# Input transposes, keys and queries of a batch five steps earlier, across the batch boundary

## The chip, the cores and the metric

The kernel runs on one core of a Trainium2 chip. The metric is the time on the device, in microseconds (us), and the median over runs. The kernel before takes 2675.65 us (three runs, 2670.8 to 2685.03).

## The reference

One transformer layer in float32 on x of 16 batches x 512 tokens x 256 features. Attention has 16 heads of 16 features; the mixture of experts has 8 experts, of which 2 are chosen for a token, and a shared one.

```python
Q, K, V = heads(Wq, bq), heads(Wk, bk), heads(Wv, bv)      # of layernorm(x)
scores = einsum('bhid,bhjd->bhij', Q, K) / 4
QJ = einsum('bhid,hde->bhie', tanh(Q), J_attn)
scores = scores + lambda_attn * einsum('bhie,bhje->bhij', QJ, tanh(K))
probs = softmax(where(causal, -inf, scores))
x = x + (probs @ V) @ Wo.T + bo
x = x + moe(layernorm(x))                  # router, top 2 of 8 experts, shared expert
```

## The kernel before, in words

The attention stage comes first and is the only one that the change touches. Then follow routing, a scatter, the experts (135 slots of 128 rows) and a combining stage.

**Steps.** The attention stage works through 16 batches. A batch has 16 steps (`STEPS`): four groups of four heads, and for each group four tiles of 128 keys. Every engine has its own instruction stream, written out by hand in the same order of steps: `over_batches` (L79) emits a prologue batch (`PROLOGUE`, batch number -1), batch 0, a loop of six turns over two batches each, and then batches 13, 14, 15 and a tail.

**In each step** TensorE computes *row scores* (`rows`, L449: four heads, queries as rows), from which VectorE takes each row's maximum (`maximum`, L601), and *column scores* (`cols`, L462: keys as rows), which ScalarE turns into exponentials (`exps`, L550), GpSimd masks (`select`, L735 and L737), and TensorE multiplies with the values in the next step (`pv`, L475). The row scores run seven steps (`LEAD`) ahead of the column scores. So the row scores of batch b, group 0 begin at step 9 of batch b - 1, and those of groups 2 and 3 at steps 1 and 5 of batch b; the column scores of group g begin at step 4g of batch b.

**The maxima.** The column scores have the negated maximum of each query as one more contraction row (two rows, a high and a low part), so the product comes out already shifted. The path: VectorE writes `nm` (L609, L611), TensorE transposes it (piece "mt", L404), ScalarE copies it to `mT` (L538), and SyncE issues four small DMAs, one for each head, from `mT` to rows 96 and 97 of `qs` (`max_rows`, L826). The column scores of a group wait for them (`mrow_loaded`). The "mt" piece of a group stands three steps before that group's column scores: groups 1, 2, 3 at steps 1, 5, 9, and group 0 of the next batch at step 13.

**The pieces.** Everything else that TensorE does for a batch is cut into pieces that share one PSUM bank, `ps_m`. The table `PIECES` says at which step, at which of two places of it, and for which batch relative to the current one each runs: "xt" (transposes of the normalized input `xn`, L386), "k" and "q" (L391), "qj" (tanh(Q) times J, L394), "v" (L399), "mt" (above), "ot" (transposes of the attention output, L408), "ont" (L412), "out" (L418), "gt" (L424) and "lg" (router logits, L430). A piece waits until the one before it has been taken out of `ps_m`.

**The stacks.** For exactness the scores use a split of each factor into a high and a low part. Keys and queries, and tanh(K) and tanh(Q) J, are split into four tiles (`part_kh`, `part_kl`, `part_th`, `part_tl`), which SyncE stores into DRAM (`store`, L766: `k_parts`, `q_parts`, 256 KB a DMA). From there it loads them (`load_stack`, L789) into `ks` and `qs`, where the parts of one head stand one above the other. A stack is loaded in these portions: keys of groups 0 and 1 (`load_keys01`, six DMAs of 256 KB, issued after the second "q" piece), queries of groups 0 and 1 (`load_queries01`, six of 256 KB, after the second "qj" piece; three of them, then a wait until the stores of `part_th` and `part_tl` have landed, L810, then three), and group 2 and group 3 (`load_group`, twelve DMAs of 128 KB each). One queue, SyncE's, issues all of these, the maxima's DMAs, the loads of `xn` (L841) and `xres` (L878, 512 KB each) and the stores of the result `x1_d` (L859), in program order.

**Around the boundary of the stage.** Batches 4 to 15 get their layer norm's statistics (`statistics1`, L682 and L685) in the prologue batch, from a ring of four buffers that SyncE refills (L836, 512 KB a load).

Of the kernel before, what the change touches and what calls it, by code (L numbers as in the profile page):

```python
# [31 lines left out]
NB, S, D = 16, 512, 256  # L32
H, HD = 16, 16
KT = D // P
TT = S // P
# [11 lines left out]
EARLY = 4  # L47
# [4 lines left out]
LOADS = 16 * 12  # L52
PROLOGUE, TAIL = -1, NB
SHARED_FIRST = 9
# [24 lines left out]
def over_batches(eng, batch):  # L79


    batch(Batch(0, PROLOGUE))
    batch(Batch(0, 0))
    with eng.Fori(0, NB // 2 - 2) as i:
        batch(Batch(i, 1))
        batch(Batch(i, 2))
    for last in (NB - 3, NB - 2, NB - 1, TAIL):
        batch(Batch(0, last))
# [4 lines left out]
PIECES = [  # L93
# [8 lines left out]
    (8, 0, "ont", 0, -1),  # L102
    (9, 0, "ot", 1, 0), (9, 1, "mt", 3, 0),
    (10, 0, "ont", 1, -1),
    (11, 0, "out", 0, -1),
    (12, 0, "out", 1, -1),
    (13, 0, "ot", 2, 0), (13, 1, "mt", 0, 1),
    (14, 0, "gt", 0, -1), (14, 1, "gt", 1, -1),
    (15, 1, "lg", 0, -1),
]  # L110
# [65 lines left out]
def attention_stage(nc, ctx, sbt, x_v, wqT, bq, wkT, bk, wvT, bv, woT, bo, J, lam,  # L176
# [200 lines left out]
    def _(pe):  # L377
# [101 lines left out]
        def batch(b):  # L479
            att = b.at_least(0) and b.at_most(NB - 1)  # L480
            for n in range(STEPS):
                if b.fixed and b.off == PROLOGUE and n == 8:
                    pe.wait_ge(const_ready, 2)
                rows(b, n, 0)
                if att:
                    cols(b, n, 0)
                rows(b, n, 1)
                piece(b, n, 0)
                rows(b, n, 2)
                if att:  # L490
                    cols(b, n, 1)
                rows(b, n, 3)
                if n > 0 and att:
                    pv(b, n - 1)
                if n == 0 and b.at_least(1):
                    pv(b.plus(-1), STEPS - 1)
                piece(b, n, 1)
# [4 lines left out]
    def _(act):  # L502
# [56 lines left out]
        def batch(b):  # L559
            att = b.at_least(0) and b.at_most(NB - 1)  # L560
            for n in range(STEPS):
                if b.fixed and b.off == PROLOGUE and n == 14:
                    act.wait_ge(mv1_ready, NB - EARLY)
                    nc.scalar.activation(rstd1[:, EARLY * TT:], mv1[:, EARLY * TT:, 1], ACT.Sqrt, bias=eps[:, 0:1]).then_inc(root1, 1)
                if att:
                    exps(b, n, 0)
                piece(b, n, 0)
                if att:
                    exps(b, n, 1)
                if n % TT == 0:  # L570
                    if n > 0 and att:
                        o_copy(b, n // TT - 1)
                    if n == 0 and b.at_least(1):
                        o_copy(b.plus(-1), G - 1)
                piece(b, n, 1)
# [4 lines left out]
    def _(dve):  # L580
# [107 lines left out]
        def batch(b):  # L688
            for n in range(STEPS):
                if b.fixed and b.off == PROLOGUE and n < NB - EARLY:  # L690
                    statistics1(n)
# [9 lines left out]
                piece(b, n, 1)  # L701
                if 11 <= n < 11 + TT and piece_exists(b, -1):
                    statistics(b.plus(-1), n - 11)
                if n == 9 and b.plus(2).at_most(NB - 1):
                    layer_norm(b.plus(2))
# [7 lines left out]
    def _(pool):  # L713
# [26 lines left out]
        def batch(b):  # L740
            att = b.at_least(0) and b.at_most(NB - 1)
            for n in range(STEPS):
# [3 lines left out]
                piece(b, n, 1)  # L746
                if n == 6 and piece_exists(b, -1):
                    d = b.plus(-1)
# [7 lines left out]
    def _(sp):  # L756
# [38 lines left out]
        def load_keys01(d):  # L795
# [6 lines left out]
            if d.at_least(2):  # L802
                sp.wait_ge(cols_ready, (d.v - 1) * STEPS * 2)
                sp.nop(nofuse=True)
# [26 lines left out]
        def batch(b):  # L831
            for n in range(STEPS):
                if b.fixed and b.off == PROLOGUE and n < NB - EARLY - 4:

                    sp.wait_ge(st1_ready, (n + 1) * TT)
                    sp.dma_start(ring[n % 4], x_v[EARLY + 4 + n]).then_inc(ring_loaded[n % 4], 16)  # L836
                if n == 3 and b.plus(2).at_most(NB - 1):

# [3 lines left out]
                if n == 0 and b.at_least(0) and b.at_most(NB - 1):  # L842
                    load_group(b, 3)
                for place in range(2):
                    for kind, j, d, _ in pieces_at(b, n, place):
# [10 lines left out]
                        elif kind == "out":  # L856
                            sp.wait_ge(taken["out"], count("out", j, d))
                            sp.nop(nofuse=True)
                            sp.dma_start(x_of(x1_d, d)[:, 2 * j:2 * j + 2], xres[:, 2 * j:2 * j + 2]).then_inc(x1_stored[j], 16)  # L859
                if n == 12 and b.plus(1).at_most(NB - 1):  # L860
                    load_group(b.plus(1), 2)
                if n in (9, 10, 11) and b.at_least(0) and b.at_most(NB - 2):
# [3 lines left out]
                    sp.dma_start(dest, zrows[:]).then_inc(xs_zeroed, 16)  # L866
                if n == 15 and b.at_least(0) and b.at_most(NB - 1):

# [1033 lines left out]
```

## Time and profile before

| | |
|---|---|
| median of three runs | 2675.65 us |
| profiled execution | 2675.09 us |
| its span in the trace | 2673.3 us |
| mean granted clock of TensorE | 0.877 of full speed |
| busy: TensorE, weight loads, VectorE, ScalarE, GpSimd | 78%, 55%, 51%, 38%, 28% |
| column scores, first and last start | 103.9 and 1480.3 us |
| DMA moved | 358.63 MB, mean 134 GB/s |

The span is that of the trace, from its first to its last instruction. In the rows below, L462 is line 462 of the kernel; PE is TensorE, PEld its weight loads, DVE VectorE, ACT ScalarE, POOL GpSimd and SPq SyncE's queue. The time that the trace gives for a DMA on SPq is that of its issue, not of its transfer.

### The profile page before, as it was taken

The page shows a single profiled execution, that of the slowest core. Times are in us where ns is not written, and L with a number is a line of the kernel's source. Part 1 is how long each engine was busy: PE and PEld are TensorE (multiplying, and loading weights), DVE is VectorE, ACT ScalarE, POOL GpSimd, SP SyncE. Part 2 cuts the span into 40 slices and gives each one's busy share as a digit, 9 for nine tenths or more (in the row PEclk, how much of TensorE's full clock was granted, in tenths as well). Part 3 has the DMA queues.
Part 4 walks back from the last instruction along what each step waited for, and adds up shares of the span by engine and source line. Part 5 has one row for each costly group of instructions (what it writes and reads, how often), then busy time and mean ns, then how long its engine had stood idle before and what let it go on. Part 6 is the DMA issues. An engine that isn't in the chain of part 4 may idle for free. (4 is left out here: it accounts for less than half of the span.)

```text
span 2673.3 us, 46424 instructions
## 1 busy us (share of the span) xinstructions
PE 2088.7 (78%) x11806; PEld 1478.9 (55%) x11807; DVE 1351.5 (51%) x3928; ACT 1021.7 (38%) x1784; POOL 749.9 (28%) x1095
## 2 busy tenths in 40 slices
PE   3676787769677877697779467869999999997774
PEld 1344454445444544455445356757777777775664
DVE  4555465546554655465546554434444444444655
ACT  1333343335333533353335222225555555553221
POOL 3112221222122212221222146737500000002665
PEclk9688888889788988887889679879999999998987
DMA  8776866686668676867674343433311111113675
GB/s 230 154 128 157 162 151 132 150 170 154 127 148 174 149 134 157 163 151 131 151 160 83 149 140 137 152 116 123 126 55 55 55 53 55 53 55 126 208 219 173
DMA packets 225155, 358.63 MB, mean 134 GB/s; under 512 B 28240, under 2 KB 114256, under 8 KB 224976
## 3 DMA queue, kind: packets, MB, share of 16 engines
q1 hardware_dynamic: 205776, 309.02, 49.2%
q0 software_dynamic: 15744, 46.16, 5.2%
q8 instruction: 78, 1.28, 0.2%
q10 hardware_dynamic: 3456, 1.34, 0.2%
q14 instruction: 101, 0.83, 0.1%
HBM read 210.92 MB, written 144.44 MB: 133 GB/s over the span
## 5 line engine op out<-in xcount | busy, mean ns | idle before, releaser
L601 DVE CUSTOM_DVE_ANT_0 ps_rows<-ps_rows,maskrow 128x128 f32<-128x128 f32 (+3 forms) x1024 | 489.1, 507 | 393.2 <-PE ps_rows L449 385.0
L550 ACT ACTIVATE probs<-ps_cols 128x1024 f32<-128x1024 f32 (+3 forms) x512 | 357.4, 698 | 626.1 <-PE ps_cols L462 625.9
L449 PE MATMUL ps_rows<-ks,qs 96*128 96x128 f32 (+3 forms) x1024 | 442.0, 434 | 88.6 <-DVE mx L601 50.2
L462 PE MATMUL ps_cols<-qs,ks 98*128 98x512 f32 (+3 forms) x1024 | 286.1, 364 | 222.1 <-DMA qs<-mT 222.0
L462 PEld LDWEIGHTS ps_cols<-qs,ks 98*128 98x128 f32 x1024 | 193.2, 213 | 259.5 <-issue 205.1
L735 POOL TENSOR_TENSOR pace<-eps 1x1 f32<-1x1 f32 x256 | 47.5, 186 | 998.2 <-ACT probs L550 998.2
L449 PEld LDWEIGHTS ps_rows<-ks,qs 96*128 96x128 f32 x1024 | 216.7, 212 | 185.7 <-DVE mx L601 113.4
L1708 DVE TENSOR_TENSOR h_lo<-ps_h,h_hi 128x512 fp32r<-128x512 f32 x135 | 93.4, 692 | 254.3 <-ACT h_hi L1680 254.3
L475 PE MATMUL ps_o<-probs,vt 128*32 128x512 f32 (+3 forms) x2048 | 202.6, 470 | 0.1
L1674 ACT ACTIVATE sg_e<-ps_ge 128x512 f32<-128x512 f32 x135 | 80.8, 598 | 266.5 <-PE ps_ge L1600 266.5
L1827 POOL COPY ix<-pos 128x2 int32 (+1 forms) x64 | 15.5, 241 | 552.4 <-POOLq L904 525.8
L737 POOL TENSOR_SCALAR_AFFINE_SELECT probs<-probs 128x512 f32<-128x512 f32 x256 | 160.7, 628 | 0.0
L601 DVE DVE_READ_ACCUMULATOR2_ANT mx<- 128x1 f32 x1024 | 145.4, 142 | 0.0
L1454 POOL DMA_INDIRECT xs_d<-row,idx x128 | 132.1, 1032 | 32.5 <-issue 29.0
L1831 POOL DMA_INDIRECT yr<-yo_d,ix x128 | 131.2, 1025 | 31.8 <-issue 26.1
L1036 PE MATMUL ps_g<-x2T,swg 128*128 128x512 f32 x384 | 114.6, 439 | 24.1 <-DVE x2T L1139 18.0
L1722 DVE TENSOR_TENSOR h_e<-sg_e,ps_ue 128x512 f32<-128x512 f32 x135 | 92.9, 688 | 72.9 <-PE ps_ue L1600 72.9
L1050 PE MATMUL ps_y<-swd,hT 128*128 128x256 f32 x768 | 107.0, 300 | 26.4 <-DVE hT L1130 19.8
L1085 ACT ACTIVATE sg<-ps_g 128x512 f32<-128x512 f32 x64 | 38.2, 596 | 231.1 <-PE ps_g L1036 128.6
L1050 PEld LDWEIGHTS ps_y<-swd,hT 128*128 128x128 f32 x768 | 102.9, 207 | 32.1 <-DVE hT L1130 22.3
L722 POOL TENSOR_TENSOR part_kl<-lin,part_kh 128x512 fp32r<-128x512 f32 x64 | 81.5, 1274 | 113.3 <-ACT part_kh L523 112.5
L1600 PE MATMUL ps_ue<-w_hi,x_lo 128*128 x270 | 109.9, 488 | 0.0
(201 smaller groups left out, 4035.7 us busy)
## 6 DMA issues: line engine op xcount, KB each, us to landing
ks<-k_parts SPq DMA_DIRECT2D x96, 256.0 KB, 8.7
qs<-q_parts SPq DMA_DIRECT2D x96, 256.0 KB, 12.3
ks<-k_parts SPq DMA_DIRECT2D x192, 128.0 KB, 4.6
qs<-q_parts SPq DMA_DIRECT2D x192, 128.0 KB, 7.0
xs_d<-zrows SPq DMA_DIRECT2D x45, 384.0 KB, 2.8
xr<-xs_d SPq DMA_DIRECT2D x135, 128.0 KB, 2.0
yo_d<-y_e SPq DMA_DIRECT2D x135, 128.0 KB, 1.7
xn<-in_L_attn_x_dram SPq DMA_DIRECT2D x16, 512.0 KB, 4.4
```

What stands on the lines that cost most here:

```text
L449: nc.tensor.matmul(bank[:, 0:(it + 1) * P], qs[0:STACK, hh, it * P:(it + 1) * P], ks[0:STACK, hh, 0:(it + 1) * P], start=True, stop=True). ...
L462: mm = nc.tensor.matmul(ps_cols[pair][:, e, jt * P:S], ks[0:MROW + 2, hh, jt * P:(jt + 1) * P], qs[0:MROW + 2, hh, jt * P:S], start=True, ...
L475: mm = nc.tensor.matmul(ps_o[2 * HD * h:2 * HD * (h + 1), jt * P:S], vt[:, b.par, jt, g * HG + h], probs[:, n % 2, h, jt * P:S], start=jt ...
L550: nc.scalar.activation(probs[:, n % 2, 2 * pair:2 * pair + 2, jt * P:S], ps_cols[pair][:, :, jt * P:S], ACT.Exp).then_inc(exp_done, 1)
L601: nc.vector.tensor_tensor_reduce(out=bank, in0=bank, in1=maskrow[:, (TT - 1 - it) * P:S], scale=1.0, scalar=LOWEST, op0=ALU.add, op1=ALU.m ...
L737: nc.gpsimd.affine_select(out=blk, in_=blk, compare_op=ALU.is_ge, fill=0.0, base=0, pattern=[[0, HG], [1, P]], channel_multiplier=-1).then ...
L1036: mm = nc.tensor.matmul(bank[i % 2][:], w[:, wp, k, i * P:(i + 1) * P], self.x2T[:, s.par, xp, k], start=at == 0 and k == 0, stop=at == 2 ...
L1050: mm = nc.tensor.matmul(self.ps_y[j][:, tt], self.hT[:, s.par, hp, i, t * P:(t + 1) * P], self.wd[:, wp, i], start=at == 0 and i == 0, sto ...
L1454: nc.gpsimd.indirect_dma_start(xs_d[:, :], bass.IndirectOffsetOnAxis(ap=idx[q][:, r:r + 1], axis=0), row[q][:], None).then_inc(scattered[q ...
L1600: mm = nc.tensor.matmul(bank, part[:, k], w[side][:, k * width:(k + 1) * width], start=at == 0 and k == 0, stop=at == 2 and k == n - 1)
L1708: nc.vector.tensor_tensor(h_lo[:, d.par], ps_h[:], h_hi[:, d.par].bitcast(F32), ALU.subtract).then_inc(hl_ready, 1)
L1831: nc.gpsimd.indirect_dma_start(yr[c][r][:], None, yo_d[:, :], bass.IndirectOffsetOnAxis(ap=ix[c][:, r:r + 1], axis=0))\
```

## The change

The table of pieces is rewritten. "xt", "k" and "q" go from steps 0, 2 and 3 of the batch before theirs to steps 11 to 15 of the batch two before it; "qj" goes from step 4 to step 0 and "v" from steps 6 and 7 to steps 2 and 3 of the batch before; "ont", "out", "gt" and "lg" of the preceding batch come four steps sooner. "mt" and "ot" stay. The loads and helper steps tied to them move along: the load of `xn` from step 3 to step 1, the layer norm from step 9 to 6, the statistics from 11 to 8, the bias add on `xres` from 6 to 3, its load from 15 to 13. In SyncE's stream, `load_group` of group 2 goes ahead of the pieces of step 12. A second prologue batch is added (`PROLOGUE` is now -2, `FILL` -1), in which the statistics of later batches run. The maxima still go by DMA.

```diff
-PROLOGUE, TAIL = -1, NB
+PROLOGUE, FILL, TAIL = -2, -1, NB
...
-    batch(Batch(0, PROLOGUE))
-    batch(Batch(0, 0))
+    for first in (PROLOGUE, FILL, 0):
+        batch(Batch(0, first))
...
 PIECES = [
-    (0, 0, "xt", 0, 1), (0, 1, "xt", 1, 1),
+    (0, 0, "qj", 0, 1), (0, 1, "qj", 1, 1),
     (1, 0, "ot", 3, -1), (1, 1, "mt", 1, 0),
-    (2, 0, "k", 0, 1), (2, 1, "k", 1, 1),
-    (3, 0, "q", 0, 1), (3, 1, "q", 1, 1),
-    (4, 0, "qj", 0, 1), (4, 1, "qj", 1, 1),
+    (2, 1, "v", 0, 1),
+    (3, 1, "v", 1, 1),
+    (4, 0, "ont", 0, -1),
     (5, 0, "ot", 0, 0), (5, 1, "mt", 2, 0),
-    (6, 1, "v", 0, 1),
-    (7, 1, "v", 1, 1),
-    (8, 0, "ont", 0, -1),
+    (6, 0, "ont", 1, -1),
+    (7, 0, "out", 0, -1),
+    (8, 0, "out", 1, -1),
     (9, 0, "ot", 1, 0), (9, 1, "mt", 3, 0),
-    (10, 0, "ont", 1, -1),
-    (11, 0, "out", 0, -1),
-    (12, 0, "out", 1, -1),
+    (10, 0, "gt", 0, -1), (10, 1, "gt", 1, -1),
+    (11, 0, "lg", 0, -1), (11, 1, "xt", 0, 2),
+    (12, 0, "xt", 1, 2), (12, 1, "k", 0, 2),
     (13, 0, "ot", 2, 0), (13, 1, "mt", 0, 1),
-    (14, 0, "gt", 0, -1), (14, 1, "gt", 1, -1),
-    (15, 1, "lg", 0, -1),
+    (14, 0, "k", 1, 2), (14, 1, "q", 0, 2),
+    (15, 0, "q", 1, 2),
 ]
...
-                if b.fixed and b.off == PROLOGUE and n < NB - EARLY:
+                if b.fixed and b.off == FILL and n < NB - EARLY:
                     statistics1(n)
...
-                sp.wait_ge(cols_ready, (d.v - 1) * STEPS * 2)
+                sp.wait_ge(cols_ready, ((d.v - 2) * STEPS + 2 * TT) * 2)
...
-                if n == 3 and b.plus(2).at_most(NB - 1):
+                if n == 1 and b.plus(2).at_least(1) and b.plus(2).at_most(NB - 1):
 
                     sp.wait_ge(ready["xt"], (b.v + 2) * 2)
...
                 if n == 0 and b.at_least(0) and b.at_most(NB - 1):
                     load_group(b, 3)
+                if n == 12 and b.plus(1).at_least(0) and b.plus(1).at_most(NB - 1):
+                    load_group(b.plus(1), 2)
...
-                if n == 12 and b.plus(1).at_most(NB - 1):
-                    load_group(b.plus(1), 2)
...
-                if n == 15 and b.at_least(0) and b.at_most(NB - 1):
+                if n == 13 and b.at_least(0) and b.at_most(NB - 1):
```

SyncE's stream, from the load of the key stack of groups 0 and 1 to the maxima's DMAs, in batch 0. Before (`16x8x512` is a load of two groups, 256 KB; `16x4x512` one of a single group, 128 KB):

```order
L789 DMA ks<-k_parts 16x8x512 x6
L766 DMA q_parts<-part_th 128x512
L766 DMA q_parts<-part_tl 128x512
L766 DMA q_parts<-part_th 128x512
L766 DMA q_parts<-part_tl 128x512
L789 DMA qs<-q_parts 16x8x512 x6
L826 DMA qs<-mT 2x512 x8
L866 DMA xs_d<-zrows 128x768 x3
```

After, the same stretch, which now begins at the end of the batch before:

```order
L789 DMA ks<-k_parts 16x8x512 x6
L789 DMA ks<-k_parts 16x4x512 x6
L789 DMA qs<-q_parts 16x4x512 x6
L766 DMA q_parts<-part_th 128x512
L766 DMA q_parts<-part_tl 128x512
L766 DMA q_parts<-part_th 128x512
L766 DMA q_parts<-part_tl 128x512
L789 DMA qs<-q_parts 16x8x512 x6
L841 DMA xn<-in_L_attn_x_dram 128x4x256
L826 DMA qs<-mT 2x512 x12
```

The eight maxima's DMAs before are those of groups 2 and 3, and group 1's have gone out ahead of this stretch; the twelve after are those of groups 1, 2 and 3. Group 3's loads and that of `xn` now stand inside the stretch.

TensorE's stream after the change, steps 14 and 15 of a batch and the first step of the loop's body:

```order
L391 MATMUL ps_m<-xT,wq 128x512 x2
L449 MATMUL ps_rows<-ks,qs 128x384
L462 MATMUL ps_cols<-qs,ks 128x128 x2
L449 MATMUL ps_rows<-ks,qs 128x384
L391 MATMUL ps_m<-xT,wq 128x512 x2
L449 MATMUL ps_rows<-ks,qs 128x384
L462 MATMUL ps_cols<-qs,ks 128x128 x2
L449 MATMUL ps_rows<-ks,qs 128x384
L475 MATMUL ps_o<-probs,vt 32x256 x4
L84 UNCONDITIONAL_BRANCH
```

The two query pieces now stand one at the end of step 14 and one in the middle of step 15, just ahead of the loop's start; before, they stood together in step 3.

## Rows read from the trace of the kernel before

**Rows 1.** The page, part 2: busy tenths in 40 slices of the span.

```profile
PE   3676787769677877697779467869999999997774
DMA  8776866686668676867674343433311111113675
```

**Rows 2.** The waits of line 462: what ended TensorE's idle time before it.

```profile
  DMA qs<-mT: 266.7, 23
```

**Rows 3.** Timeline of TensorE, steps 3 to 8 of one batch (start, us, instruction, idle before).

```profile
652.81 1.98 PE L391 MATMUL ps_m<-xT,wq 128*128 128x512 f32 x4
654.23 0.80 PE L449 MATMUL ps_rows<-ks,qs 96*128 96x512 f32 x1
...
659.78 0.59 PE L449 MATMUL ps_rows<-ks,qs 96*128 96x128 f32 x1
...
664.24 0.36 PE L449 MATMUL ps_rows<-ks,qs 96*128 96x256 f32 x1
...
668.42 0.53 PE L449 MATMUL ps_rows<-ks,qs 96*128 96x384 f32 x1
...
673.24 0.58 PE L449 MATMUL ps_rows<-ks,qs 96*128 96x512 f32 x1
687.77 1.22 PE L462 MATMUL ps_cols<-qs,ks 98*128 98x512 f32 x2 [13.95 <-DMA qs<-mT]
```

**Rows 4.** The same timeline: the stalls of batches 0 and 14, and a short one between.

```profile
155.83 1.22 PE L462 MATMUL ps_cols<-qs,ks 98*128 98x512 f32 x2 [12.36 <-DMA qs<-mT]
...
185.61 1.22 PE L462 MATMUL ps_cols<-qs,ks 98*128 98x512 f32 x2 [2.39 <-DMA qs<-mT]
...
1400.35 1.22 PE L462 MATMUL ps_cols<-qs,ks 98*128 98x512 f32 x2 [15.48 <-DMA qs<-mT]
```

**Rows 5.** Timeline of SyncE's queue: the first batch and the batch of rows 3.

```profile
128.55 2.77 SPq L789 DMA_DIRECT2D ks<-k_parts  x6
...
658.99 2.72 SPq L789 DMA_DIRECT2D ks<-k_parts  x6
...
664.35 13.48 SPq L789 DMA_DIRECT2D qs<-q_parts  x6
677.93 2.43 SPq L826 DMA_DIRECT2D qs<-mT  x4
```

**Rows 6.** The waits of SyncE's queue (us in total, times, longest).

```profile
SPq L810 <- DMA q_parts<-part_tl: 179.0, 32, 11.2
```

**Rows 7.** The DMA engines from 680 to 700 us, in 40 slices of 0.5 us.

```profile
DMA  9999999998762000000000000000000000000001
```

**Rows 8.** Timeline of all engines around the first row scores.

```profile
78.66 0.66 PE L449 MATMUL ps_rows<-ks,qs 96*128 96x128 f32 x2 [20.23 <-DMA qs<-q_parts]
...
81.61 0.27 DVE L601 CUSTOM_DVE_ANT_0 ps_rows<-ps_rows,maskrow 128x128 f32<-128x128 f32 x1
```

**Rows 9.** Windows: engines' busy time, PEclk, DMA share, GB/s.

```profile
0.00:100.00 100.00, 35.91 (x72) 17.42 (x73) 48.54 (x196) 12.32 (x19) 22.43 (x23) 0.78 0.79 197
...
635.00:640.00 5.00, 5.00 (x26) 3.42 (x24) 3.34 (x11) 3.68 (x5) 0.77 (x2) 0.57 1.08 166
...
650.00:655.00 5.00, 5.00 (x22) 2.44 (x22) 2.70 (x10) 3.08 (x7) 4.90 (x6) 1.00 0.87 329
...
680.00:685.00 5.00, 0.00 (x0) 0.00 (x0) 0.00 (x0) 0.00 (x0) 0.00 (x0) 0.50 1.02 124
...
661.00:686.50 25.50, 10.95 (x69) 7.34 (x69) 8.49 (x33) 3.89 (x7) 4.62 (x7) 0.81 1.02 163
```

**Rows 10.** Timeline of all engines at the loop's back edge.

```profile
723.85 4.73 SPq L789 DMA_DIRECT2D ks<-k_parts  x6
...
724.72 0.79 PE L449 MATMUL ps_rows<-ks,qs 96*128 96x512 f32 x1 [3.59 <-issue]
```

**Rows 11.** Groups of instructions from 78 to 1480 us: key and query pieces.

```profile
L391 PE MATMUL ps_m<-xT,wq 128*128 128x512 f32 x120 | 59.5, 618 | 4.0 <-DVE lin L624 4.0
L391 PE MATMUL ps_m<-xT,wk 128*128 128x512 f32 x120 | 59.5, 618 | 4.1 <-ACT mT L538 4.1
```

More of the change, by code:

```diff
@@ L481, in batch @@
             for n in range(STEPS):
-                if b.fixed and b.off == PROLOGUE and n == 8:
+                if b.fixed and b.off == FILL and n == 8:
                     pe.wait_ge(const_ready, 2)
@@ L561, in batch @@
             for n in range(STEPS):
-                if b.fixed and b.off == PROLOGUE and n == 14:
+                if b.fixed and b.off == FILL and n == 14:
                     act.wait_ge(mv1_ready, NB - EARLY)
@@ L701, in batch @@
                 piece(b, n, 1)
-                if 11 <= n < 11 + TT and piece_exists(b, -1):
-                    statistics(b.plus(-1), n - 11)
-                if n == 9 and b.plus(2).at_most(NB - 1):
+                if 8 <= n < 8 + TT and piece_exists(b, -1):
+                    statistics(b.plus(-1), n - 8)
+                if n == 6 and b.plus(2).at_least(1) and b.plus(2).at_most(NB - 1):
                     layer_norm(b.plus(2))
@@ L746, in batch @@
                 piece(b, n, 1)
-                if n == 6 and piece_exists(b, -1):
+                if n == 3 and piece_exists(b, -1):
                     d = b.plus(-1)
@@ L832, in batch @@
             for n in range(STEPS):
-                if b.fixed and b.off == PROLOGUE and n < NB - EARLY - 4:
+                if b.fixed and b.off == FILL and n < NB - EARLY - 4:
                     sp.wait_ge(st1_ready, (n + 1) * TT)
                     sp.dma_start(ring[n % 4], x_v[EARLY + 4 + n]).then_inc(ring_loaded[n % 4], 16)
-                if n == 3 and b.plus(2).at_most(NB - 1):
+                if n == 1 and b.plus(2).at_least(1) and b.plus(2).at_most(NB - 1):
                     sp.wait_ge(ready["xt"], (b.v + 2) * 2)
```

## The prediction

> **What bounds the kernel now.** I read the page first, then the waits of TensorE's column scores, then the timelines of TensorE and of SyncE's queue over one batch, then the DMA rates in short windows. The page shows an attention stage of some 1400 us in which no engine is full and a long stage after it that the change does not touch [rows 1]. The waits of the column scores (L462) name one cause above all: 266.7 us of idle time end with the maxima's DMA, `qs<-mT` [rows 2]. The timeline of one batch shows where: TensorE is ready for group 2's first column scores at about 673.8 us and starts them at 687.77, an idle time of 13.95 us [rows 3]. The same stall is there in each of batches 0 to 14, between 12.4 and 15.9 us, from 155.83 to 1400.35 us; the mean of the 15 is 14.4 [rows 4]. The spacing of these stalls is (1400.35 - 155.83) / 14 = 88.9 us a batch.
>
> SyncE's queue tells why the maxima are late [rows 5]. At 658.99 it issues six key loads (1.57 MB), then four query-side stores (1.05 MB), then the first three query loads; then it waits for the stores to land. The six query issues take 13.48 us, and the waits of this kind sum to 179.0 us over 32, nearly all in one wait per batch [rows 6]. Only then, at 677.93, do the four small DMAs of group 2's maxima go out, and they land at about 687.5. The DMA engines are full from 680 until 684.5 and run dry near 686.5, just before TensorE goes on [rows 7]. So two things are in series ahead of the maxima: an issue queue in program order, and 4.19 MB that must pass first. From the key loads' issue to the column scores it takes 28.8 us here, 27.3 in the first batch, and 29.35 in the mean of the 15 [rows 3 to 5].
>
> **The moved pieces, one by one.** No arithmetic is added. Transposes, keys and queries of a batch go to steps 11 to 15 of the batch two before it, their products with J to step 0, values to steps 2 and 3; the tail of the batch before comes three to four steps sooner. The rows have the new query loads at step 9 as before, so they now have nine steps of slack, not five; but they did not wait for them in the loop (the only such wait is 20.2 us before the very first scores [rows 8]), and so this slack is worth nothing. What matters is what stands ahead of the maxima. Maxima of groups 1, 2, 3, 0 keep steps 1, 5, 9, 13 and their three steps of lead. Before, group 2's stood behind key loads, J-side stores and query loads. Now group 1's do, and SyncE's order puts two more things between: the twelve loads of group 3 (they follow the key loads at step 0) and the load of `xn` (step 1, ahead of the maxima). Group 2's become free. So **the stall moves from step 8 to step 4 and its queue grows.**
>
> Size of the growth. Group 3's loads are twelve of 128 KB, 1.57 MB. In the stretch where such loads run the engines are full and move 166 GB/s [rows 9], so 9.5 us. `xn` is 0.52 MB; stores and contiguous loads make up the 329 GB/s of one window [rows 9], so 1.6 us, and at 166 GB/s it would be 3.2; I take 2. Together 11.5 us. The bounds: nothing, were the engines to have room for it, and 15.9 us (1.57 MB at the 124 GB/s of a window in which only the last query loads run [rows 9], 12.7, and 3.2). I take 11.5, as the row of 166 GB/s is that of the same loads. The maxima then land 29.35 + 11.5 = 40.9 us after the key loads' issue.
>
> The Trainium skill (DMA: Bandwidth & Descriptors, section Bandwidth) gives 425 GB/s for long loads, and 6.15 us for one of 1 MB. As estimates from that page, the added 2.1 MB would take 5 us by the first and 13 by the second. The rows of this case (166 GB/s, engines full) speak against the first, and they decide.
>
> How long TensorE has other work after the key loads' issue: before, 673.8 - 658.99 = 14.8 us. After, from the start of the second query piece to that issue there are 6.2 us (652.81 to 658.99 [rows 3, 5]), and TensorE has left: the rest of step 15, 3.7 (between 2.5 and 5: steps are 4 to 5 us long and the piece starts a good us after the first row scores); step 0 with the J pieces, 659.78 - 654.23 = 5.55; step 1, 664.24 - 659.78 = 4.46 less a wait of 0.9 for a J piece that step 1 no longer follows, some 4.0; steps 2 and 3 with the value pieces, 4.2 and 4.8, as steps 6 and 7 were [rows 3]. Sum 22.3 + 0.6 for the row scores ahead of the column scores, less 6.2: 16.7. The stall is then 40.9 - 16.7 = 24.2 us, against 14.4: **+9.8 us in each of 15 batches, +147 us.**
>
> What is given back. At the loop's back edge (six times) TensorE idles 3.6 us here, and about 4 in the mean, without a cause in the profile, and SyncE's key issues take 4.73 us instead of 2.7 [rows 10]. Now that gap falls between the key loads' issue and the stall, so it shortens the stall: 6 x 4 = -24 us. Key and query pieces are spread over four steps and no longer come in pairs; TensorE's waits for the bias adds that drain them sum to 4.0 us and for `mT` 4.1 [rows 11]: -8 us at most.
>
> The boundary. Statistics of the later batches now run in the second prologue batch, so their ring loads of 512 KB stand behind the first query loads: before the first maximum, at 81.6 us, the load of index 9 had only the query loads ahead [rows 8]; now five ring loads and `xn` follow those, five loads of 0.52 MB more than before, at the 197 GB/s of the first 100 us [rows 9] 2.6 us each: +13, less 3 for an earlier start. Batch 1's transposes, keys and queries (some 10 us of TensorE, at the 1.98 us of a piece [rows 3]) then run beside the first row scores, where no column scores run yet, and no longer in batch 0: I take -6 us. Net +4.
>
> At step 12 group 2's loads and the first key stores now go ahead of group 0's maxima: 1.57 MB at 166 GB/s and 1.05 MB at 329, 12.7 us, within the some 18 us of steps 12 to 15 and hence free; before, they waited at most 2.4 us there, in batch 1 [rows 4].
>
> Sum against the profiled execution's own 2675.09 us (span 2673.3, and 0.6 below the median of the runs): +147 - 24 - 8 + 4 = +119, so 2675 + 119 = **2794 us.**
>
> **The rivals.** *The queue is longer than the sum* (slower still). Steps 12 to 15 now issue group 2, all key stores, `xres`, query stores and the key loads, and any backlog pushes the key loads back; then group 0's maxima stall as well. For it: the engines' share is six to eight tenths in this stage already [rows 1]. Against: up to the key loads' issue about 21 us of transfers stand in 22 us. Were 5 us more lost per batch: 2794 + 75 = 2869.
>
> *The extra loads hide* (the other side). If the key loads pass while TensorE still works on steps 0 to 3, and group 3's 128 KB loads use time in which the engines wait for stores to land, the landing stays at 29.35 us after the issue while TensorE's own work is 16.7 rather than 14.8 us, and the stall falls to 12.7: 15 x -1.7 = -26, with -24, -8 and +4: 2675 - 54 = 2621, faster. It decides where the extra 11.5 us shrink below 54 / 15 = 3.6 us. Against it: there is no gap from 661 to 686 in the engines' share, which is 1.02 as this view counts it [rows 9].
>
> *Maxima overtake.* Their DMA has two rows only. If they passed the large transfers once issued, `xn` and the last query loads would cost them nothing more, and the growth would be that of the wait for the stores, 9.5 less the 1.9 us of added work: 15 x 7.6 = 114, and with -28 the time is 2761. Against it, here the maxima land only when the engines run dry [rows 7]. The Trainium skill (DMA: Bandwidth & Descriptors, section Queues, rings and completion order) says that an engine takes descriptors in ring order but that completion is not first in, first out over an issuing engine; by that such overtaking is possible.
>
> *Loads at the stores' pace.* If the added 2.1 MB passed at 329 GB/s, they would take 6.4 us: 15 x (6.4 - 1.75) = 70, and with -28 the time is 2717. Against it stands every window in which loads alone run, 124 to 166 GB/s [rows 9]. The Trainium skill's 425 GB/s (DMA: Bandwidth & Descriptors, section Bandwidth) is a case of this kind.
>
> *The change does not do what it says*: the stall stays one of 14.4 us because some wait I have not seen holds the steps in place, 2675 within 10 us.
>
> **How the numbers follow.** Forecast (stall moved and longer, 2735 to 2855) 0.61; loads at the stores' pace 0.05; maxima that overtake 0.08; longer queue and a second stall 0.14; hidden loads 0.08; no change 0.04. The unknowns are the added transfer (9 to 15.9 us, so 15 x -2.5 and +4.4: -38 and +66), the time left of step 15 (1.3 us, so 20) and the back edge (24). The range is 2735 to 2880: the low end takes the first two together (2794 - 58), the high end is past the longer queue's 2869. A measurement of this kernel tells 0.5%, some 13 us, from no change. Slower by more than that 0.88, within it 0.04, faster 0.08.
>
> **What would show it.** In the profile after: in L462's waits `qs<-mT` with a sum of 340 to 420 us, not 266.7; one wait a batch, at group 1's first column scores (the maxima's DMAs of groups 2 and 3 come after it), of about 24 us, or 20 after a back edge; the query issues at about 17 us rather than 13.5; group 3's issues between key loads and J stores; and a first maximum near 90 us. The forecast is wrong if the wait at step 4 is under 18 us, if the batch spacing stays below 92 us (I expect 88.9 + 119 / 15 = 96.8), or if another wait of over 3 us a batch appears, at group 0's maxima or at `stack23`.

## The result, and the profile after

| | before | after |
|---|---|---|
| median of four runs each, same chip | 2673.23 us (2664.87 to 2685.03) | 2803.0 us (2786.58 to 2811.91) |
| ratio, 95% interval | | 1.0478 [1.0431, 1.0525] |
| profiled execution, span | 2675.09, 2673.3 us | 2808.22, 2806.5 us |
| granted clock of TensorE, mean | 0.877 | 0.866 |
| column scores, first to last start | 1376 us | 1482 us |

The change makes the kernel slower by 4.8%. It takes away no arithmetic and adds none, so the first view to read is that of the waits that grew. The waits of line 462 after (us, times):

```profile
  DMA qs<-mT: 433.4, 20
```

The waits of SyncE's queue after (us, times, longest):

```profile
SPq L810 <- DMA q_parts<-part_tl: 209.6, 32, 15.2
```

The first was 266.7 us in 23 waits [rows 2], the second 179.0 [rows 6]. The view of a line adds the waits of TensorE's matmuls and of its weight loads, which can be waits in the same stall; the matmuls alone waited 222.0 us before and 355.4 after, and these sums are used in the table of experiments. The timeline of TensorE after (start, us, instruction, idle time before it) has the stalls of batches 0, 1 and 14, and between them that of the batch shown next:

```profile
161.23 1.22 PE L462 MATMUL ps_cols<-qs,ks 98*128 98x512 f32 x2 [24.51 <-DMA qs<-mT]
...
257.29 1.22 PE L462 MATMUL ps_cols<-qs,ks 98*128 98x512 f32 x2 [27.59 <-DMA qs<-mT]
...
713.36 0.58 PE L449 MATMUL ps_rows<-ks,qs 96*128 96x512 f32 x1
740.23 1.22 PE L462 MATMUL ps_cols<-qs,ks 98*128 98x512 f32 x2 [26.29 <-DMA qs<-mT]
...
1504.38 1.22 PE L462 MATMUL ps_cols<-qs,ks 98*128 98x512 f32 x2 [24.18 <-DMA qs<-mT]
```

There are 15 such stalls, one a batch, all at the first column scores of group 1 (step 4), and none is left at step 8. Their mean is 23.6 us (sum 354.3), against 14.4 before [rows 4]. Five of them follow a back edge of the loop (a loop of six turns jumps back five times) and have a mean of 19.4; the other ten have 25.7. The spacing is (1504.38 - 161.23) / 14 = 95.9 us a batch, from 88.9.

SyncE's queue over the same batch after shows what stands ahead of the maxima:

```profile
698.32 5.53 SPq L789 DMA_DIRECT2D ks<-k_parts  x12
703.89 2.77 SPq L789 DMA_DIRECT2D qs<-q_parts  x6
706.75 0.37 SPq L766 DMA_DIRECT2D q_parts<-part_th  x1
...
708.79 18.23 SPq L789 DMA_DIRECT2D qs<-q_parts  x6
727.34 0.41 SPq L841 DMA_DIRECT2D xn<-in_L_attn_x_dram  x1
727.92 2.43 SPq L826 DMA_DIRECT2D qs<-mT  x4
```

This is the order of the change's fence: key loads of groups 0 and 1 with the first six of group 3 (x12), the other six of group 3, four stores, the queries, `xn`, and only then the maxima. The query issues take 18.23 us, most of it the wait of L810 for the stores; they took 13.48 [rows 5]. From the key loads' issue to the column scores it is 740.23 - 698.32 = 41.9 us here and 40.9 in the mean of the 15. All that time the DMA engines are full. Their share from 700 to 740 us, in 40 slices of 1 us, after:

```profile
DMA  9999999999999999999999999999999999999990
```

Before the loop, the first maximum and the wait behind it on TensorE, and the ring loads on SyncE's queue that cause it, after (timeline of all engines):

```profile
68.03 20.59 SPq L836 DMA_DIRECT2D probs<-in_L_attn_x_dram  x6
...
91.96 0.27 DVE L601 CUSTOM_DVE_ANT_0 ps_rows<-ps_rows,maskrow 128x128 f32<-128x128 f32 x1
92.34 0.72 PE L449 MATMUL ps_rows<-ks,qs 96*128 96x128 f32 x2 [12.74 <-DVE mx L601]
```

It starts at 91.96 us, 10.3 later than before [rows 8]. The first column scores start at 119.0, 14.7 later.

How little of this is work shows in the windows of the attention stage, from first to last column scores (us, busy time with counts of TensorE, weight loads, VectorE, ScalarE and GpSimd, then PEclk, DMA share, GB/s). The kernel before:

```profile
104.00:1481.00 1377.00, 1046.71 (x5928) 668.99 (x5928) 735.60 (x2647) 559.10 (x908) 342.95 (x615) 0.86 0.71 147
```

And after:

```profile
119.00:1602.00 1483.00, 1025.87 (x5916) 655.77 (x5918) 730.40 (x2644) 553.44 (x897) 336.77 (x610) 0.84 0.68 135
```

TensorE has the same work (1047 and 1026 us busy) and 457 us without work in place of 330. The DMA share *falls* from 0.71 to 0.68: the same bytes over a longer stage. The granted clock goes down with it, 0.86 to 0.84.

### The profile page after: what moved, and what is told of

It is laid out like the page before. It is cut to its first block and busy times, and to the rows that moved or that the text cites. A ratio compares the mean times of both kernels' runs of the same rounds, so it can differ in the third digit from the quotient of the medians.

```text
span 2806.5 us, 46452 instructions
## 1 busy us (share of the span) xinstructions
PE 2072.7 (74%) x11738; PEld 1468.0 (52%) x11807; DVE 1348.7 (48%) x3928; ACT 1022.3 (36%) x1784; POOL 746.2 (27%) x1095
## 5 line engine op out<-in xcount | busy, mean ns | idle before, releaser
L462 PE MATMUL ps_cols<-qs,ks 98*128 98x512 f32 (+3 forms) x1024 | 280.5, 358 | 355.4 <-DMA qs<-mT 355.4
L462 PEld LDWEIGHTS ps_cols<-qs,ks 98*128 98x128 f32 x1024 | 190.8, 211 | 393.2 <-issue 301.4
L1827 POOL COPY ix<-pos 128x2 int32 (+1 forms) x64 | 15.6, 243 | 550.7 <-POOLq L904 524.1
L1050 PE MATMUL ps_y<-swd,hT 128*128 128x256 f32 x768 | 116.9, 315 | 45.6 <-DVE hT L1130 27.4
L1050 PEld LDWEIGHTS ps_y<-swd,hT 128*128 128x128 f32 x768 | 110.8, 221 | 54.1 <-issue 41.2
```

The lines of the kernel that those rows point to most:

```text
L462: mm = nc.tensor.matmul(ps_cols[pair][:, e, jt * P:S], ks[0:MROW + 2, hh, jt * P:(jt + 1) * P], qs[0:MROW + 2, hh, jt * P:S], start=True, ...
L1050: mm = nc.tensor.matmul(self.ps_y[j][:, tt], self.hT[:, s.par, hp, i, t * P:(t + 1) * P], self.wd[:, wp, i], start=at == 0 and i == 0, sto ...
```

## The experiments

The theory: the maxima's four small DMAs are late because of what stands ahead of them in SyncE's one stream, by bytes and by the wait at L810; so whatever is moved behind them shortens the stall by its own time. The rivals: the queue is a matter of total DMA load (then order does not matter), or the stall is a matter of the issuing engine alone (then another engine's queue removes it), or the new slack of the queries buys nothing (then nothing done to the loads beats the kernel before). Each ratio is to the kernel before on the same chip (medians of before: 2661.38 us beside a_xn to a_kq, 2588.16 beside a_kq3 to b_q5, 2601.13 beside the rest). The columns of waits are sums over TensorE's matmuls in its timeline, in us: column scores waiting for `mT`, and row scores waiting for `q_parts` (without the one before the very first row scores). They and the last column come from traces of different chips; the kernel before itself has 222 and 1376 on one and 210 and 1361 on another.

| kernel | ratio [95%] | waits for `mT` | waits for queries | first to last column scores |
|---|---|---|---|---|
| before (first chip) | | 222 | 0 | 1376 |
| after (first chip) | 1.0478 [1.0431, 1.0525] | 355 | 0 | 1482 |
| a_xn | 1.0464 [1.0417, 1.0512] | 333 | 0 | 1461 |
| a_g3 | 1.0239 [1.0185, 1.0293] | 225 | 50 | 1416 |
| a_q5 | 1.0322 [1.0272, 1.0372] | 171 | 115 | 1432 |
| a_kq | 0.9758 [0.9707, 0.9809] | 29 | 115 | 1278 |
| a_kq3 | 0.9746 [0.968, 0.9812] | 142 | 0 | 1275 |
| a_act | 1.0173 [1.014, 1.0206] | 56 | 1 | 1389 |
| b_act | 1.0194 [1.0144, 1.0244] | 17 | 147 | 1390 |
| b_q5 | 0.9803 [0.9771, 0.9835] | 51 | 98 | 1302 |
| a_act_x | 0.9918 [0.9892, 0.9944] | 68 | 35 | 1331 |
| a_kqs | 0.9415 [0.938, 0.9449] | 67 | 1 | 1194 |
| ctl_after | 1.0498 [1.0467, 1.053] | 355 | 0 | 1481 |
| ctl_before (one run) | | 210 | 0 | 1361 |

**a_xn: the load of `xn` behind the maxima.** In the changed kernel, SyncE's step 1 issues it ahead of the pieces; here behind them.

```diff
-    if n == 1 and b.plus(2).at_least(1) and b.plus(2).at_most(NB - 1):
...
-        sp.dma_start(xn[:], x_of(x_v, b.plus(2))).then_inc(x_loaded, 16)
...
+    if n == 1 and b.plus(2).at_least(1) and b.plus(2).at_most(NB - 1):
...
+        sp.dma_start(xn[:], x_of(x_v, b.plus(2))).then_inc(x_loaded, 16)
```

> The changed kernel with the load of xn moved behind group 1's maxima. Queue theory (everything issued ahead of the maxima must pass first): one load of 0.52 MB less, so the stall at step 4 falls by 1.6 to 3.2 us in each of 14 batches: 2803 - 22 to 45, some 2770, and the layer norm does not become late. Rival (the stall is set by the wait for the stores alone, and what is issued after it costs nothing): no change, 2800.

Measured: the stalls have a mean of 22.2 us, 1.4 less than after's 23.6, just under the 1.6 to 3.2 expected; the two traces are of different chips, and the kernel before's mean stall differs by 0.6 between two chips (14.4 and 13.8). The times don't settle it either: 1.0464 against 1.0478 and 1.0498 of the changed kernel, with intervals of half a per cent. So `xn` is a small term of the queue, as the sum had it (2 of 11.5 us), and this run by itself proves no more than that.

**a_g3: group 3's twelve loads behind the maxima.** They go from the head of step 0 to the end of step 1, after its pieces.

```diff
-    if n == 0 and b.at_least(0) and b.at_most(NB - 1):
-        load_group(b, 3)
...
+    if n == 1 and b.at_least(0) and b.at_most(NB - 1):
+        load_group(b, 3)
```

> The changed kernel with group 3's twelve loads moved behind group 1's maxima. Queue theory: the maxima land 9.5 us sooner, so the mean stall falls from 23.6 to about 14 us, that of the kernel before; but the row scores of step 5 then wait for group 3's loads, some 6 us. Net 3.5 us a batch: about 2750. Rival (these loads hid in free time of the DMA engines): the stall stays at 23 us and step 5 waits as well, so slower, 2860 or more.

Measured 1.0239. TensorE's timeline of a_g3:

```profile
691.42 1.22 PE L462 MATMUL ps_cols<-qs,ks 98*128 98x512 f32 x2 [16.13 <-DMA qs<-mT]
698.20 0.47 PE L449 MATMUL ps_rows<-ks,qs 96*128 96x128 f32 x1 [1.99 <-DMA qs<-q_parts]
```

The stall's mean is 15.0 us, 8.6 less than after: the price of 1.57 MB ahead of the maxima, forecast as 9.5. The late loads bring a new wait at the row scores of step 5, which use them: 1.3 to 4.8 us, 8.0 in the last batch, 3.1 in the mean. This settles where the growth of the stall came from (9.8 us forecast, 9.2 measured): with group 3's loads put back behind the maxima, the stall is nearly the old one again, and half of the 4.8% is gone.

**a_q5: queries at the end of step 5, behind group 2's maxima**, still four steps ahead of their use. Batch 0 keeps the old place, here and in the edits below.

```diff
-    if (kind, j) == ("qj", 1):
+    if (kind, j) == ("qj", 1) and d.fixed and d.off == 0:
         load_queries01(d, 0)
         load_queries01(d, 1)
...
+    if n == 5 and b.at_least(0) and b.plus(1).at_most(NB - 1):
+        load_queries01(b.plus(1), 0)
+        load_queries01(b.plus(1), 1)
```

> The changed kernel with the query loads of groups 0 and 1 moved from step 0 to step 5, behind the maxima of groups 1 and 2. Queue theory: 1.57 MB and the wait for the stores leave the way of group 1's maxima, so the stall falls from 23.6 to about 11 us; the queries still land by step 9, as five of the nine steps of slack suffice. 2803 - 15 x 12.5 = 2615, faster than the kernel before. Rival (slack of the queries is worth nothing, because whatever is moved stalls elsewhere): the wait comes back at the row scores of step 9, 2750 or more.

The stall fell as expected (mean 11.4 us, 11 expected). The time did not. Timeline of TensorE, then of SyncE's queue, of a_q5:

```profile
703.51 1.22 PE L462 MATMUL ps_cols<-qs,ks 98*128 98x512 f32 x2 [14.89 <-DMA qs<-mT]
730.64 0.47 PE L449 MATMUL ps_rows<-ks,qs 96*128 96x128 f32 x1 [7.50 <-DMA qs<-q_parts]
```

On the queue:

```profile
689.32 26.09 SPq L826 DMA_DIRECT2D qs<-mT  x7
715.64 2.70 SPq L789 DMA_DIRECT2D qs<-q_parts  x6
```

The loads leave at 715.64 us and the row scores of step 9 wait for them: 7.5 us here, 115 in all. Between the stall and step 9 TensorE has work for only 730.64 - 7.50 - 703.51 = 19.6 us; the loads leave 12.1 us after the stall and take 15.0 more. The DMA engines from 700 to 740 us of a_q5, in slices of 1 us, with their GB/s:

```profile
DMA  9920000000000000499999999999996000000000
GB/s 392 360 83 0 16 0 0 0 0 0 0 0 0 0 8 12 96 197 109 111 107 152 107 152 109 111 102 133 129 238 252 16 0 0 0 0 0 0 8 8
```

They idle for 13 us and then run one kind of load at 107 to 111 GB/s in six of the slices, more in others; 1.57 MB in 15.0 us is 105. My expectation took the slack to be there in steps; in microseconds, on this side of the stall, it isn't. The rival (a wait takes its place) was right in kind.

**a_kq: keys at the end of step 1 as well, queries at step 5.**

```diff
-    if (kind, j) == ("q", 1):
+    if (kind, j) == ("q", 1) and d.fixed and d.off == 0:
         load_keys01(d)
...
+    if n == 1 and b.at_least(0) and b.plus(1).at_most(NB - 1):
+        load_keys01(b.plus(1))
```

> The changed kernel with the key loads of groups 0 and 1 moved from step 15 to step 1, behind group 1's maxima, and the query loads to step 5, behind group 2's. Queue theory: ahead of group 1's maxima stand only group 3's loads, the J-side stores and xn, some 17 us, which is about TensorE's own work up to step 4; no stall of over 2 us at the maxima, and some 3 us at the row scores of step 9, which wait for the queries. 2803 - 15 x 20.5 = about 2495. Rival (the DMA engines are the bound, so the bytes cost their time wherever they stand): the batch stays above 84 us and the time above 2620.

Measured 0.9758 (2595.45 us), between the theory's number and the rival's, and nearer to the rival's. The waits for `mT` are down to 29 us in all, as the theory had it, but row scores wait for the queries 7.2 to 8.0 us in each batch (3 expected), the 115 us of a_q5 again. So the order of this one stream takes the changed kernel from 4.8% slower to 2.4% faster, with no byte less. That excludes total load as the cause of the 4.8%; how far below this the bytes let the time come, it doesn't tell.

**a_kq3: keys at step 1, queries at the end of step 3.** The edit is a_kq's with `n == 3` for the queries.

> As a_kq, with the query loads at the end of step 3, ahead of group 2's maxima. In a_kq the row scores of step 9 waited 7.7 us for them, since they are issued some 10 us before TensorE needs them and take 14 us. Queue theory: issued five to seven us earlier, they land by step 9, and group 2's maxima, now behind them, wait 1 to 3 us at step 8. Ratio to the kernel before 0.976 - 15 x 5 / 2661 = about 0.947. Rival (the bytes are the bound, the wait only changes its name): 0.97 to 0.98 again, with a wait of some 7 us at step 8.

Measured 0.9746, no better than a_kq. The timeline of TensorE in a_kq3, at steps 4 and 8 of one batch:

```profile
795.00 0.72 PE L462 MATMUL ps_cols<-qs,ks 98*128 98x512 f32 x2 [3.24 <-DMA qs<-mT]
818.74 1.21 PE L462 MATMUL ps_cols<-qs,ks 98*128 98x512 f32 x2 [9.47 <-DMA qs<-mT]
```

The rows' wait is gone, and 142 us of waits for `mT` are back: 1 to 5 us at step 4, and 4 to 11 at step 8, for now the query loads stand ahead of group 2's maxima. A miss: I had put the queries between two sets of maxima and counted only the first.

**a_act and b_act: ScalarE issues the maxima's DMAs**, right after it has copied them to `mT`, in the changed kernel and in the kernel before.

```diff
     nc.scalar.activation(mT[0:2 * HG], ps_m[0:2 * HG], ACT.Copy).then_inc(taken[kind], 1)
+    act.wait_ge(taken["mt"], d.v * G + j + 1)
+    for h in range(HG):
+        act.dma_start(qs[MROW:MROW + 2, slot(d, j) + h].bitcast(F32), mT[2 * h:2 * h + 2, :].bitcast(F32))\
+            .then_inc(mrow_loaded, 16)
...
-    elif kind == "mt":
-        max_rows(d, j)
```

> The changed kernel with the maxima's DMAs issued by ScalarE, right behind its copy, everything else as it is. If the stall is the order of SyncE's stream and ring alone, the maxima land within some 3 us and the stall of 23.6 us goes: 2803 - 350, ratio about 0.925, with ScalarE's four issues of each group (64 groups) costing up to 1 us each, 0.95. If the maxima on another queue still have to pass the bytes that are in the DMA engines already, they land some 21 us after the key loads' issue and a stall of about 5 us stays: 0.95 to 0.975. Rival (the wait is not SyncE's but one for DMA bandwidth): above 1.0.

> The kernel before with the maxima's DMAs issued by ScalarE. The stall of 14.4 us at step 8 goes, but the queries of groups 0 and 1 still land 29 us after the key loads' issue, and the row scores of step 9 need them some 4 us after step 8: a wait of about 9 us at the row scores takes its place. Net 5 us a batch, ratio about 0.97, clearly slower than a_act: this is what the five steps of slack are worth once the maxima no longer queue. Rival (the slack is worth nothing in any order): the same ratio as a_act.

Both were misses in time. The waits for `mT` fell from 355 to 56 us in a_act, some 3.5 a batch, and to 17 in b_act. The ratio above 1.0 is the number of a_act's rival, but not its reason. Where the stall went is in the timelines of the three engines in a_act, in one batch:

```profile
654.47 5.51 SPq L793 DMA_DIRECT2D ks<-k_parts  x12
661.33 2.43 ACTq L541 DMA_DIRECT2D qs<-mT  x4
674.07 1.22 PE L462 MATMUL ps_cols<-qs,ks 98*128 98x512 f32 x2 [4.14 <-DMA qs<-mT]
```

ScalarE issues the maxima 8.6 us after the key loads in the mean of 15 batches, where SyncE came to it after 29.1. But once issued they are no faster. By the landing events of the trace they land 9.7 us after their last issue in a_act and 9.2 in the changed kernel (7.2 in b_act and 7.6 in the kernel before), and 20.7 us after the key loads' issue in a_act: the expectation's second case, in which they still have to pass the bytes that are in the DMA engines already (some 21 us, a stall of about 5). The engines are full meanwhile (share 1.07 and 148 GB/s from 661 to 674 us), and of all that had been issued before them only the last three to five DMAs landed later than they did. So the own queue saves the maxima what stands ahead of them in SyncE's stream (the stores, the wait at L810, the query loads, `xn`), and hardly anything of the transfers already issued.

The Trainium skill (DMA: Bandwidth & Descriptors, section Queues, rings and completion order) says that each DMA engine takes turns between the queues that have work for it. The trace agrees only in so far as a few DMAs were passed: by turns alone one would expect the maxima to land soon after their issue, and they took 9.7 us. Where that time goes is not shown. Its section Issuing engines are not separate DMA queues says that DMAs of all issuing engines run on the same 16 DMA engines, and that issuing from several saves only the time to initiate, usually small. The first half fits what is seen here; the second leaves out the waits in the stream, which are what was saved.

The two ratios, 1.0173 and 1.0194, lie within each other's intervals. By b_act's expectation that is its rival's sign (slack worth nothing in any order). It doesn't settle that, for in a_act a second wait took the place of the first. The second wait shows in the waits of all engines of a_act (us, times, longest):

```profile
PE ps_rows L449 <- DVE mx L605: 139.3, 97, 12.6
ACT probs L554 <- PE ps_o L475: 118.6, 46, 2.7
```

VectorE waits for `xn` (117.4 us over 15), and TensorE for VectorE's maxima. The second row is mostly ScalarE's own issuing: its idle time of up to 2.7 us stands where it issues the four DMAs, which take it 2.4 us. In b_act the row scores of step 9 wait 10 us for the queries in each batch, as its expectation said (about 9), though the ratio of 0.97 did not come; timeline of TensorE of b_act:

```profile
783.55 0.47 PE L449 MATMUL ps_rows<-ks,qs 96*128 96x128 f32 x1 [11.14 <-DMA qs<-q_parts]
```

**a_act_x: a_act, and the load of `xn` one step sooner**, first in step 0 (`n == 0` in place of `n == 1`), to tell the `xn` wait from ScalarE's own cost.

> The maxima by ScalarE's queue, and the load of xn issued first in step 0, ahead of group 3's loads. In the run with the maxima on ScalarE alone, VectorE waited 8.2 us for xn at step 6, and TensorE 6 us for VectorE's maxima: a load that had hidden under the stall. If that is so, these 6 us go and the ratio falls from 1.017 to about 0.983. Rival (the cost of that version is ScalarE's 2.4 us of issuing in each of 64 groups, in the way of the exponentials): above 1.0 still.

Measured 0.9918, near. VectorE's wait for `xn` is 5.0 us in all, TensorE's for maxima 51 in place of 139, and the stage is 58 us shorter (on another chip). It is also clearly below b_act's 1.0194: with the `xn` wait gone, the new table with maxima from ScalarE beats the old one, each against before on its own chip. What stays beside a_kqs (1331 against 1194 us of stage, same chip) was not taken apart by a run. ScalarE's issuing, 64 times 2.4 us or some 150 us, is one candidate: TensorE waits 29 us for `onT` and 17 for `probs` in this stage of a_act_x, against 3 and 0 in a_kqs. Another 35 us are waits for queries. And the same matmuls keep TensorE busy for 1091 us against 1024, at a mean granted clock of 0.87 against 0.93 (the mean alone does not give this: the changed kernel has 1026 us at 0.84). In a_act_x ScalarE still has:

```profile
ACT probs L554 <- PE ps_o L475: 121.2, 47, 2.7
```

**b_q5: the kernel before, queries behind group 2's maxima** (the edit of a_q5 at the end of step 5, where its maxima go out).

> The kernel before with the query loads of groups 0 and 1 moved behind group 2's maxima (end of step 5). The stall at step 8 falls from 14.4 to about 3 us, and the row scores of step 9 wait for the queries, 8 us or more: ratio 0.98 to 1.0. Rival (the position of the query loads does not matter): 1.0 with the stall at step 8 unchanged.

Measured 0.9803, the low end of what was expected. Timeline of TensorE of b_q5, steps 8 and 9:

```profile
733.58 0.72 PE L462 MATMUL ps_cols<-qs,ks 98*128 98x512 f32 x2 [3.05 <-DMA qs<-mT]
744.14 0.47 PE L449 MATMUL ps_rows<-ks,qs 96*128 96x128 f32 x1 [7.78 <-DMA qs<-q_parts]
```

The stall of 14 us becomes two, of 0.4 to 4.7 us and of 4.7 to 9.1 (mean 6.5). That is what the reordering gives with the old table of pieces.

**a_kqs: keys at step 1, the queries' first half at step 3 and second at step 5.** Each half stands behind a set of maxima, and the first half still has time before step 9.

```diff
+    if n == 1 and b.at_least(0) and b.plus(1).at_most(NB - 1):
+        load_keys01(b.plus(1))
+    if n in (3, 5) and b.at_least(0) and b.plus(1).at_most(NB - 1):
+        load_queries01(b.plus(1), (n - 3) // 2)
```

> Key loads at the end of step 1, the first half of the query loads at the end of step 3 and the second at the end of step 5, behind group 2's maxima. Ahead of group 2's maxima then stand 0.79 MB less, so the waits of 5 to 9 us at step 8 fall to under 2, and the second half, issued 10 us before step 9 and 7 us long, lands in time: 6 us a batch less than with all query loads at step 3, ratio about 0.94. Rival (the bytes are the bound): 0.97 to 0.98 again.

Measured 0.9415 [0.938, 0.9449], 2445.12 against 2601.13 us: the best of all, faster than both kernels, and as forecast. The waits at step 8 did not all fall to under 2 us: they reach 5.4, and step 4 has 0.8 to 4.1. Waits of L462 in a_kqs:

```profile
  DMA qs<-mT: 83.7, 30
```

The waits of its SyncE queue:

```profile
SPq L810 <- DMA q_parts<-part_tl: 11.5, 2, 10.1
```

SyncE's queue over steps 0 to 3 of one batch in a_kqs (x6 at 660.23 are group 3's):

```profile
660.23 2.77 SPq L789 DMA_DIRECT2D qs<-q_parts  x6
...
665.70 0.39 SPq L841 DMA_DIRECT2D xn<-in_L_attn_x_dram  x1
668.62 2.44 SPq L826 DMA_DIRECT2D qs<-mT  x4
671.56 2.70 SPq L789 DMA_DIRECT2D ks<-k_parts  x6
674.50 1.25 SPq L789 DMA_DIRECT2D qs<-q_parts  x3
```

The maxima leave at 668.62, three microseconds after the last issue ahead of them; the keys follow. The wait for the stores' landing is gone from the stream too (11.5 us, from 209.6): by the time the queries' turn comes, the stores have landed. The window of its attention stage:

```profile
117.00:1312.00 1195.00, 1024.25 (x5920) 651.29 (x5920) 728.26 (x2645) 549.79 (x898) 335.89 (x610) 0.93 0.82 168
```

TensorE has 171 us without work (1195 less 1024), the DMA share is 0.82, and the mean granted clock 0.93.

**ctl_after and ctl_before: both kernels again, on the chip of a_kqs and a_act_x.**

> The changed kernel once more, unedited, on the chip that also runs the next three. Ratio 1.048 again, within 0.005, and the mean stall at step 4 of 23 to 24 us, if the difference lies in the kernel; less of both if this chip's DMA moves the stacks faster.

> The kernel before, unedited, for a trace from the same chip. Mean stall at step 8 of 14.4 us and a batch of 88.9 us; if the chip's DMA is faster, both are smaller, and the difference to the changed kernel's batch stays near 7 us.

The ratio repeats (1.0498), and so do the stalls: mean 23.7 and 13.8 us, spacing 95.4 and 87.7.

## Why the prediction was right

By its steps:

- **The stall moves to step 4 and grows.** Forecast 24.2 us for a stall without a back edge, measured 25.7 in the mean of those ten, and 23.6 over all 15. Sum of the stalls: +137.8 us (354.3 less 216.5), forecast +147 - 24 = +123 with the back edges.
- **Its two sides.** From the key loads' issue to the column scores 41.3 us in the ten without a back edge (40.9 over all 15), forecast 40.9. TensorE's own work meanwhile, 41.3 less 25.7 = 15.6 us, forecast 16.7. The added transfers were 11.5 us in the sum; a_g3 puts group 3's part at 8.6 (9.5 forecast) and a_xn that of `xn` at 1.4 (2 forecast), 10.0 together. What is left of it was not taken apart; the wait for the stores at L810 grew by 2.0 us a batch (209.6 less 179.0, over 15).
- **The back edge.** Forecast 4 us off the stall, six times; measured 25.7 - 19.4 = 6.3, five times, so 31 us in place of 24. The sign and the mechanism hold; the count was one too high and the size short. TensorE's own idle time at the back edge is 3.4 us in the mean after (3.5 before, where I had about 4), so some 3 us of the 6.3 are something else that no run took apart.
- **Pieces spread and hidden** (-8 and -6). By the last column scores the stage is 121 us later: +14.7 before the first ones, +137.8 from the stalls, -4.4 from short waits for `mT` that went. 148 in all, so some 27 us came back elsewhere, more than the 14 forecast; no run took that rest apart.
- **The prologue.** First maximum at 92 us, forecast 90. Net +14.7 at the first column scores where I had +10 for the loads; the -6 of hidden work lies within the 27.
- **Sum.** Forecast 2794 us, range 2735 to 2880; measured 2803.0. The profiled execution also has 12 us more after the attention stage; the control pair has 4 less there, so that is not the change's. The spacing was 95.9 us, 96.8 forecast; `qs<-mT` at L462 433 us, forecast 340 to 420, a little above.
- **Luck in the sum.** By the last column scores the change costs 121 us where the sum had 119, and that closeness is in part luck: the stalls were 15 us dearer and the start 5, while short waits gave back 4 and the rest 13 more than forecast. The mechanism does not rest on it: the place of the stall, its size and what stands ahead of it were each seen by themselves.

The rivals: *the extra loads hide* needed a gap in the DMA engines, and their row shows none from 700 to 739 us. *Maxima overtake* fails within one queue (they land as the engines run empty, and in 14 of the 15 stalls everything issued before them had landed), and nearly so across queues (a_act, where they passed three to five DMAs at most). That a_g3 and a_q5 shorten the stall by 8.6 and 12.2 us fits the queue, but this rival too had a shorter wait for the stores, so it is the landings that decide. *A longer queue* needed a second stall, and there is only one a batch. *Loads at the stores' pace*: group 3's 1.57 MB cost 8.6 us, that is 183 GB/s, not 329. The Trainium skill's 425 GB/s, measured for 16 MB over 128 partitions (DMA: Bandwidth & Descriptors, section Bandwidth), is not reached in these loads.

One sentence of the prediction was right for this kernel and would mislead as a rule: the queries' extra slack "is worth nothing". It is worth nothing while the loads keep their place in the stream. Once they stand behind the maxima, the slack can hide them; that it is what does so is argued, not shown: the same kind of reordering gave 0.9803 with the old table and 0.9415 with the new one, though b_q5 moves the queries alone and a_kqs the keys too, so the 4% between them is not the table's alone.

## What to carry to other kernels

Find the small transfer that a compute engine waits for, and list what stands ahead of it in its queue, bytes and waits alike, in the order of issue: the queue in order explained the old stall and the new one, and, counted again afterwards, the waits that the reorderings left. Another engine's queue spares the small transfer the issues and waits ahead of it in the stream; the bytes that are in the DMA engines already cost it the same as before (9.7 us from issue to landing in a_act, 9.2 in the changed kernel). Slack gained by an earlier schedule is only worth something when the loads are also moved behind what is urgent; a table of steps moved as one block keeps, or worsens, the order among its DMAs. And measure slack in microseconds of the steps that will be there afterwards, not in steps: when the stall went, so did the time in which the queries used to load (a_q5, a_kq3).

## What the runs showed of the hardware

- **Query loads alone run at some 109 GB/s with the DMA engines shown as full** (the rows of a_q5 above). Each of these DMAs writes 16 partitions. The Trainium skill (SBUF — State Buffer, section Door 1: The DMA port swizzle) gives 4 of 16 ports and about 109 GB/s for partitions 0 to 15. The row agrees. It is no bound for several loads in flight: group 3's, of 16 partitions each too, passed at 183 GB/s (a_g3). What sets the rate of such a mix was not tried. I had missed the page in the prediction, where it would have been the better ground for the slow loads.
- **A DMA's issue costs an engine about 0.6 us** in this form: four small ones took 2.43 us on SyncE and 2.4 on ScalarE. On ScalarE that is 64 x 2.4 = 154 us of an engine with other work.
- **A second issuing queue did not shorten the way through the DMA engines.** With the engines full, the maxima's four DMAs landed 9.7 us after their last issue on ScalarE's queue (a_act, mean of 15) and 9.2 on SyncE's (after); with the engines free, 1.1.
- **The chips differ**, by 3% in the kernel before (2673, 2661, 2588, 2601 us). Of the 75 us between the first trace and ctl_before's, 14 lie in the attention stage (1376 and 1361) and some 60 behind it. Ratios are safe only beside a run of before on the same chip.
- **The granted clock is lower where TensorE stalls more**: over the attention stage its mean over the two levels (2.4 and 1.2 GHz; 0.50 in a window of the stall [rows 9]) is 0.84 with 457 us of TensorE without work, 0.86 with 330, 0.93 with 171.
